# Preparing the two-part weights in the first stage instead of ahead of the experts, with stores, loads and the end put in another order

## The reference, cut to what matters

```python
# f 1, attention without softmax
h = layernorm(X, ln_w, ln_b); Q, K, V = split(h @ W_in + b_in)       # 512 -> 3 x 512
Q, K = rope(Q), rope(K)                                              # on half of the features
A = sum over tokens of (K / |K|) * V                                 # one row of 512 per sequence
Y = (A * Q) @ W_out + b_out + X
# f 2, experts: 8, the best 2 of each token, H = 256, and a shared one, 512 wide
gates = softmax of the top 2 of xf @ gate_w
routed = sum over the two of gate * (gelu(xf @ w1[e] + b1[e]) @ w2[e] + b2[e])
shared = gelu(xf @ shared_w1 + shared_b1) @ shared_w2 + shared_b2
```

## Time and profile before

| | us |
|---|---|
| median of three runs | 1025.62 |
| the profiled execution | 1027.98 |
| its span, first to last instruction | 1025.8 |
| PE / DVE / ACT / POOL busy | 896.8 / 628.3 / 442.0 / 404.4 |
| first stage, to about | 316 |
| second stage, to about | 566 |
| between, to the first expert matmul | 657.3 |
| third stage, to about | 909 |
| fourth stage, to the end | 1025.8 |

### The profile page before, as it was taken

The page is one execution under the profiler, slowest core; times in us unless marked ns, Lnnn a source line. Parts: engine busy times, 40 slices in busy tenths (PEclk is TensorE's granted clock), DMA queues, the critical chain, the costliest instruction groups (busy, mean ns, idle before and its releaser), DMA issues.

```text
span 1025.8 us, 14729 instructions
## 1 busy us (share of the span) xinstructions
PE 896.8 (87%) x4562; PEld 739.3 (72%) x4562; DVE 628.3 (61%) x1356; ACT 442.0 (43%) x830; POOL 404.4 (39%) x337
## 2 busy tenths in 40 slices
PE   1999999999997699999999748499999999969883
PEld 1877787787785467777778537488988988857662
DVE  5656766676664775656665587366665666655653
ACT  4134233433423124122242645366666666653462
POOL 3356446545631400000000000277677777730464
PEclk9999999999998889999999878799999999989886
DMA  9122644545337568645424650678778878789496
GB/s 314 45 81 105 244 143 161 188 158 200 135 144 306 190 239 312 227 165 215 154 83 169 215 151 32 238 144 149 140 147 163 154 146 149 147 176 350 62 160 107
DMA packets 78074, 174.68 MB, mean 170 GB/s; under 512 B 10841, under 2 KB 19289, under 8 KB 73137
## 3 DMA queue, kind: packets, MB, share of 16 engines
q1 hardware_dynamic: 52096, 124.60, 33.6%
q0 software_dynamic: 20592, 45.96, 25.1%
q10 hardware_dynamic: 5312, 3.18, 1.3%
HBM read 103.68 MB, written 80.53 MB: 180 GB/s over the span
## 4 chain that ended last, share of the span: by engine, by line
PE 70%; DVE 11%; issue 7%; ACT 4%; POOL 3%; DMA 2%; SPq 1%; POOLq 0%; ACTq 0%; DVEq 0%
PE bank L1434 12%; PE bank L1435 12%; PE bank L1436 12%; PE bank L1626 3%; PE bank L1628 3%; PE bank L1627 3%; PE bank L1643 3%; PE bank L1645 3%; PE bank L1644 3%; PE bank L1613 3%; PE bank L1429 3%; POOL out L1413 2%; DVE we L1061 2%; PE bank L1635 2%; ACT hb L535 1%
## 5 line engine op out<-in xcount | busy, mean ns | idle before, releaser
L1385 POOL DMA_INDIRECT f_scratch<-ro,dst x71 | 113.2, 1595 | 48.7 <-SPq L513 23.2
L1377 POOL DMA_INDIRECT xr<-n_scratch,ids x72 | 71.1, 987 | 90.9 <-issue 65.6
L1434 PE MATMUL bank<-wkv_hi,h_hi 128*128 128x512 f32 x256 | 101.1, 395 | 3.8 <-issue 3.8
L1436 PE MATMUL bank<-wkv_hi,h_lo 128*128 128x512 f32 x256 | 100.7, 393 | 0.0
L1435 PE MATMUL bank<-wkv_lo,h_hi 128*128 128x512 f32 x256 | 100.6, 393 | 0.0
L1188 DVE TENSOR_TENSOR ro<-bank,b2b 128x512 f32<-128x512 f32 x71 | 49.1, 692 | 70.3 <-PE bank L1645 70.3
L1626 PE MATMUL bank<-we,x_hi 128*128 x284 | 86.4, 304 | 0.0
L1628 PE MATMUL bank<-we,x_lo 128*128 x284 | 80.7, 284 | 0.0
L1627 PE MATMUL bank<-we,x_hi 128*128 x284 | 80.6, 284 | 0.0
L544 ACT ACTIVATE sq<-kb 128x512 f32<-128x512 f32 x32 | 20.3, 633 | 134.2 <-DVE kb L845 134.2
L1344 POOL TENSOR_TENSOR zr<-zv,half 128x4 f32<-128x4 f32 x8 | 8.1, 1009 | 137.7 <-DVE zv L961 137.7
(11 more groups left out here) (232 smaller groups left out, 2514.2 us busy)
## 6 DMA issues: line engine op xcount, KB each, us to landing
xg<-in_X SPq DMA_DIRECT2D x16, 1024.0 KB, 9.1
q_scratch<-qh SPq DMA_DIRECT2D x8, 1024.0 KB, 3.9
q_scratch<-qb SPq DMA_DIRECT2D x8, 1024.0 KB, 7.1
expert_scratch<-in_w SPq DMA_DIRECT2D x16, 512.0 KB, 7.1
q_hi<-q_scratch SPq DMA_DIRECT2D x8, 1024.0 KB, 4.7
q_lo<-q_scratch SPq DMA_DIRECT2D x8, 1024.0 KB, 6.9
out<-z SPq DMA_DIRECT2D x8, 1024.0 KB, 5.1
n_scratch<-n SPq DMA_DIRECT2D x8, 1024.0 KB, 6.4
```

The source lines that it names most:

```text
L1377: pool.indirect_dma_start(xr[u][:, :], None, n3_dram, bass.IndirectOffsetOnAxis(ids[:, i:i + 1], 0)).then_inc(row_in[u], 16)
L1385: pool.indirect_dma_start(f_dram, bass.IndirectOffsetOnAxis(dst[:, i:i + 1], 0), ro[i % NRO][:, :], None, compute_op=ALU.add).then_inc(r_s ...
L1434: pe.matmul(dst, hi(k), w_hi(k), start=(k == 0), stop=False)
L1436: last = pe.matmul(dst, lo(k), w_hi(k), start=False, stop=(k == KD - 1 and not more))
```

## The change

1. **Weights in the first stage.** The 16 expert matrices and four halves of the two shared ones are 20 "units" of 128 x 1024 (512 KB). In groups 1 to 5, four units each, a unit is loaded into one of three buffers, split by ACT (`unit_hi`) and DVE (`unit_lo`), and both parts are stored. `copy_expert` and the copies of the shared weights go.
2. **No splits later.** Experts' parts are loaded ready made (2 MB for each expert instead of 1 MB), two halves of them during steps 3 and 4. `split_s`, `split_expert`, `expert_lo` and the splits of `c1` and `c2` go.
3. **Bias row** `bo` is loaded and split at the start, and its matmul takes `ones_f` instead of `bo_one`.
4. **Fills** begin in step 1: `EARLY` is (0, 2, 4, 6, 7), and `shared_h(6)` moves into step 7. `shared_o(7, 0)` and `(7, 1)` go ahead of the batches, the other two behind the batches 2 and 5.
5. **Outputs of group six** are copied to four places of their own (`fo5` to `fo8`) and stored ahead of the later expert loads. The zeros (`zero_d`) are set at the start of the second stage, in another place, and are stored in step 2 as before.
6. **End.** `late_turn` writes four banks, all loads are ordered singly, ACT splits the turned blocks ahead of the scaling, and the last group is added to by DVE from a loaded copy of the output (`x2c`, `add_x2`) and stored by SP instead of with an adding DMA by POOL.

The diff, cut to its core:

```diff
-EARLY = (1, 3, 5, 6, 7)
+EARLY = (0, 2, 4, 6, 7)
+        units = [(e, i, 0) for e in range(E) for i in range(2)] + [(E + i, 0, h) for i in range(2) for h in range(2)]
+        UB = 3
+        w_lo = [at(f"w_lo{i}", kb_, [P, UW], F32R) for i, kb_ in enumerate((128, 132, 194))]
+        w_hi = [at(f"w_hi{i}", kb_, [P, UW], F32R) for i, kb_ in enumerate((136, 140, 176))]
-        fill = {2 + i: (("h", "o")[i % 2], EARLY[i // 2]) for i in range(6)}
+        fill = {1 + i: (("h", "o")[i % 2], EARLY[i // 2]) for i in range(7)}
...
@@ sync, first stage @@
+            def load_unit(u):
+                if u >= len(units):
+                    return
+                if u >= UB:
+                    sp.wait_ge(w_stored[u % UB], 32 * (u // UB))
+                w, k = unit_in(u)
+                sp.dma_start(w_lo[u % UB][:, :]..., w).then_inc(raw_w_in[u % UB], 16)
+            def store_unit(u):
+                sp.wait_ge(unit_split, u + 1)
+                for c, w in ((0, w_hi), (1, w_lo)):
+                    sp.dma_start(unit_out(u, c), w[u % UB][:, :]...).then_inc(w_stored[u % UB], 16)
...
             for g in range(NG):
+                u = UG * (g - 1)
+                with_units = 0 <= u < len(units)
                 sp.wait_ge(h_normed, g + 1)
                 load_x(g + 2)
+                if with_units:
+                    store_unit(u)
+                    load_unit(u + 2)
                 if g >= 1:
                     store_q(g - 1)
+                if with_units:
+                    store_unit(u + 1)
+                    load_unit(u + 3)
+                    store_unit(u + 2)
+                    load_unit(u + 4)
                 if g + 1 < NG:
                     sp.wait_ge(k_rotated, GT * (g + 1))
                     load_rt(g + 1)
+                if with_units:
+                    store_unit(u + 3)
+                    load_unit(u + 5)
...
-                if 1 <= g <= 4:
-                    copy_expert(2 * g - 2)
-                    copy_expert(2 * g - 1)
...
@@ scalar, first stage @@
+            def unit_hi(u):
+                act.wait_ge(raw_w_in[u % UB], 16 * (u // UB + 1))
+                if u >= UB:
+                    act.wait_ge(w_stored[u % UB], 32 * (u // UB))
+                act.activation(w_hi[u % UB][:, :], w_lo[u % UB][:, :]..., ACT.Copy).then_inc(unit_hi_done, 1)
                     norm_k(g, j)
                     if j == 1 and g >= 1:
                         q_hi_parts(g - 1)
+                    if 0 <= UG * (g - 1) < len(units):
+                        unit_hi(UG * (g - 1) + j)
                 if g + 1 < NG:
                     front_split(g + 1, (g + 1) % 2)
...
@@ vector, first stage @@
                 kv_prod(g, 0)
+                unit_lo(g, 0)
                 v_tile(g, 1)
                 k_tile(g, 2)
                 kv_prod(g, 1)
                 if g >= 1:
                     q_lo_parts(g - 1)
+                unit_lo(g, 1)
                 v_tile(g, 2)
                 k_tile(g, 3)
                 kv_prod(g, 2)
+                unit_lo(g, 2)
                 v_tile(g, 3)
                 kv_prod(g, 3)
+                unit_lo(g, 3)
                 rotate_q(g)
...
@@ tensor, between the stages @@
-            for m in range(KS):
-                shared_h(6, m)
             n3_turn(NG - 1)
...
                 shared_h(7, m)
+            shared_o(7, 0)
+            shared_o(7, 1)
...
-                if b in (1, 4, 7, 10):
-                    shared_o(7, (b - 1) // 3)
+                if b in (2, 5):
+                    shared_o(7, 2 + (b - 2) // 3)
...
@@ sync, after the last scatter @@
-            for n, g in enumerate(f_loads):
-                sp.dma_start(f[g][:, :, :], f_groups[g]).then_inc(f_in[n // 2], 16)
-            sp.wait_ge(stored, 16 * NT)
+            load_f(EARLY[0])
+            load_n3(1)
+            load_f(EARLY[1])
+            load_f(LATE[0])
...
+            sp.dma_start(x2c[:, :, :], out_groups[LATE[2]]).then_inc(f_in[LATE[2]], 16)
+            for j in range(GT):
+                sp.wait_ge(y_added, j + 1)
+                sp.dma_start(out_tiles[GT * LATE[2] + j], f[LATE[2]][:, j, :]).then_inc(late_stored, 16)
```

More of the change, by code:

```diff
@@ L489, in _ @@
             load_expert(2)
-            for j in range(GT):
-                store_f(6, j)
+            sp.wait_ge(t2_full, t2_use(s, KD) + 1)
             sp.wait_ge(f_stored[1], 16 * f_buf_uses[1])
-            sp.wait_ge(t2_full, t2_use(s, KD) + 1)
-            load_expert(6)
+            load_expert(6, range(2, 4))
+            sp.wait_ge(x2_stored[0], 16 * NG // 2)
+            sp.wait_ge(x2_stored[1], 16 * NG // 2)
+            sp.wait_ge(f_stored[3], 16 * f_buf_uses[3])
+            load_expert(1)
             sp.wait_ge(s_full, h_use(7, KS - 1) + 1)
@@ L497, in _ @@
             sp.dma_start(b1b[:, :, :].rearrange("p e h -> p (e h)"), b1.rearrange("e h -> (e h)").partition_broadcast(P))\
-              .then_inc(bias_in[0], 16)
-            for j in range(GT):
+              .then_inc(bias_in, 16)
+            for j in range(GT - 1):
                 store_f(7, j)
@@ L599, in _ @@
                     keep_acol(0)
+                if g == GB + 2:
+                    for u in range(UB):
+                        act.wait_ge(w_stored[u], 32 * u_uses[u])
                     scale_wo(0)
@@ L782, in _ @@
                     gelu_c(i, m)
-                for g, j in y_of[what, i, m]:
-                    normed(g, j)
                 if what == "h" and m == KS - 1 and i + 1 < len(LATE):
@@ L787, in _ @@
                         nc_hi_part(i + 1, k)
+                for g, j in y_of[what, i, m]:
+                    normed(g, j)
             normed(*y_order[-1])
@@ L1142, in _ @@
                    .then_inc(hot_marked, 1)
-                if b in (4, 7, 10, 13):
-                    f_out(7, (b - 4) // 3)
-                if b == 9:
-                    expert_lo((7,))
+                for j in {2: (0, 1), 5: (2,), 8: (3,)}.get(b, ()):
+                    f_out(7, j)
             dve.wait_ge(ids_full, 1)
@@ L1370, in _ @@
             pool.wait_ge(gates_stored, 16)
-            for u in range(3):
+            pool.wait_ge(zero_stored, 16 * (len(LATE) + 1))
+            for u in range(4):
                 pool.wait_ge(f_stored[u], 16 * f_buf_uses[u])
@@ L1554, in shared_o @@
                 n = o_use["o", g, j]
+                if g == h_order[0] and j == 0:
+                    pe.wait_ge(s_in[1], 32)
                 pe.wait_ge(hs_split, h_use(g, KS - 1) + 1)
```

338 lines of the change are left out of this document (172 added, 166 removed).

## The result

| | median of the runs, us | range | ratio to the kernel before, 95% interval |
|---|---|---|---|
| before, same chip | 1024.88 | 1023.91 to 1026.31 | |
| changed | 1040.67 | 1039.59 to 1042.88 | 1.0156 [1.0134, 1.0178] |

Slower by 16 us where 5.5 less were forecast, and outside the range (994 to 1037). The profiled execution of the changed kernel took 1039.59 us, its fastest, with a span of 1037.8; that of the kernel before took 1027.98, longer than any run in the table. So the spans are only 12.0 apart, and against the forecast 17.5 us of them are to be found.

What follows compares the result with a forecast made beforehand. PE was taken as full in the first stage (289.24 of 304 us), with later idle time behind a DVE and ACT chain holding the weight splits. -38.5 - 21 + 54 = -5.5, so 1020.1 us; range 994 to 1037.

Steps and rivals of the forecast that it cites:

- Part 1: First stage: units delay ACT's `front_split` behind a queued load; 10.7 us a group, +54 us over five groups.
- Rival C: First stage: the wait for unit u+3 is longer than forecast, time 1034 to 1041 us; chance 0.20.
- the slower access to HBM: First stage, loads behind 3 MB of stores: up to 1.8 us more a group, the kernel 9 us later.
- Part 2: Second stage: no wait for `bo`, and the turn of step 7 comes at 531.6 for 536.53, -4.9 us.
- a filled step is (536.53 - 383.78)/5 = 30.55: Second stage: six filled steps of 30.55 us each lead from 348.3 to the turn of step 7.
- the signs of being wrong: Five groups under 8 or over 12 us each, or first expert matmul not 33 to 42 us sooner without them.
- parts 2 and 3: Second stage up to the counts: -4.9 us by the turn of step 7, -18.6 in all by PE's second half.
- Part 4: Marks, lists, first tile: marks take 23.9 us, lists come 33.4 us sooner, first expert matmul 38.5 sooner in all.
- Rival D: Gathers: they wait for `store_f(7, 3)` behind 2 MB of biases, 8 us late, time 1028 us; chance 0.10.
- Part 5: The end: late products start 3.1 us sooner, run 13.8 shorter, and the tail is 4.2 shorter; -21 us.
- PE's 24 products and turns last 75.4: The end: PE's late products and turns take 75.4 us instead of 89.2, with fewer waits and cold restarts.

Runs made afterwards that it cites:

- x1: Changed kernel with 40 unread matmuls put into PE's wait in the turns of groups 2 to 6: 1032.73 us, ratio 1.0073 to the kernel before.
- e1: Changed kernel with each group's fourth unit split behind the turned blocks and Q biases (ACT) and the rotation and next statistics (DVE): 1007.57 us, ratio 0.9781.
- b2: Kernel before with three unused VectorE subtractions behind the last K-V product of groups 1 to 5: 1051.08 us, ratio 1.0203.
- e3: Changed kernel with the 4 MB of zeros issued in step 1 of the second stage instead of step 2: 1038.98 us, ratio 1.0087.
- b1: Kernel before with the 4 MB of zeros issued in step 3 of the second stage instead of step 2: 1031.99 us, ratio 1.0067.
- e4: Changed kernel with the second late group's normed rows loaded on ACT's queue instead of SP's: 1042.30 us, ratio 1.0121.
- e8: Changed kernel with one low part behind Q's, three behind the next statistics, zeros in step 1, late rows on ACT's queue: 989.18 us, ratio 0.9612.
- e5: Changed kernel with three low parts behind the last K-V product, the fourth behind the next statistics: 1005.92 us, ratio 0.9803.
- b3: Kernel before with three unused VectorE subtractions behind the next group's statistics in groups 1 to 5: 1034.99 us, ratio 1.0057.
- e2: Changed kernel with unit u+1's store and unit u+3's load issued ahead of the Q stores on SP: 1029.22 us, ratio 0.9989.

## Why the prediction was wrong

**Part 1 was right in mechanism and nearly in size.** ACT in front of `front_split`, behind a load behind stores: 11.3 us a group instead of 10.7, with waits of 9.9 to 10.5 where I had 9.1, and 1.2 or more for the clock where I had 1.6 (`x1`). The load is in 11.5 us after SP's first issue of Q (131.33 to 142.8), where I had 10.9. The period is 47.3 to 48.9, 47 was forecast. Rival C, to which I gave 0.20, asked for over 11.9 a group; it did not come. Nor does any row show the slower access to HBM that I had cited from the Trainium skill (DMA: Bandwidth & Descriptors, Latency and other measured facts) as a part of it: the first 1 MB of Q still lands 3.9 us after its issue at 131.33, as in the earlier trace rows, with the loads and stores of units around it. But the account of the wait was too simple. I followed DVE's low parts only as far as the load and called it the one cause. With the load out of the way (`e1`) 22 of the 56.5 us stay, which K tile 3 costs by being late, with the clock behind it. And I took DVE's busy time as harmless since it was not full, and each of its low parts at 1.2, where one in each group takes 2.31 beside GpSimd. `b2` shows 3.7 us a group of it, in a gap of 7 us, costing 19.9 us.

**Part 2: the step that failed is "a filled step is (536.53 - 383.78)/5 = 30.55".** I took it as the mean over five steps of the kernel before and laid it over six of the changed one. In that mean the 4 MB of zeros fell in a step with no store of f. The change brings the fills one step forward and leaves the zeros in step 2, which now holds `store_f(0, *)`. DVE waits 9.25 us for one of two buffers, PE 4.46, and the step is 37.75. That is 7.2 of the 17.5 us, and `e3` and `b1` show it from both sides. With it one of the signs of being wrong came: without the 56.5 of the first stage the first expert matmul is 27.6 us sooner, not 33 to 42. The rest of parts 2 and 3 held: the wait on `bo` gone, the next one on `q_lo` in its place (3.8 us forecast, 3.79 in the trace), the product moved out, the turn of group 7.

**Part 4 was 2.8 short.** The gates came as forecast; the marks took 25.5 us (652.41 to the lists at 677.92) where I had 23.9, and from the first gather (679.79) to the first expert matmul it was 6.5 where I had 5.6. No experiment went after this, and the cause stays open. Rival D did not occur: GpSimd's gathers start 1.9 behind the lists, as forecast.

**Part 5: the other step that failed is "PE's 24 products and turns last 75.4".** They last 86.4. I priced `n3c[1]` behind the last scatter at 0.9; it costs a wait of 5.92 in place of the 4.40 that the change removes. `e4` takes it away and gets to 83.2 (1031.1 less 947.9, by the same 8.0 behind DVE's last bank). So the other 7.8 of the 11.0 are not that load. They are short waits: PE is busy 75 us there and stands the remaining 8, most of it in waits of 1.8 to 2.3 on `hc_lo` or on issue. I had written that the change takes the wait on `hc_lo` away; it is shorter (2.16 and 2.26, one of them in place of 3.45), not gone. My figure was the busy time. Partly against it, the tail behind DVE's last bank is 8.0 us instead of 12.9. The chain of the last tile takes 5.5 (DVE's last add ends at 1035.34) where I had 4.4, but the store and the close take 2.5 and not 8.3: a plain store of 256 KB lands 2.0 us after its issue where I had 4, and no run shows the 4.3 that I put down for the program's close.

**In sum**, of 17.5 us the zeros are 7.2, the load of the late rows 3.2, the other waits of the end 7.8 less 4.9 of its tail and 1.9 ahead of it, part 4 2.8, the first stage 2.5 and the rest 1.0 (17.7 with the rounding). The zeros alone take the sum from -5.5 to about the time of the kernel before, and the end does the rest. The gains of the change without its first stage are real: 44.4 us in the trace, and `e8` keeps most of them and the corrections. A range that reached 3.7 us further would have held the time. Its upper end was built from the terms with an unknown price, while the terms that failed were those that I took as known.

## What to carry to other kernels

When work moves by one step in a software pipeline, list all that stands in the queue of each step it enters, for a mean over the old steps hides a transfer that used to fall where nobody waited. Idle time of VectorE is free only where GpSimd is idle as well and where the next thing behind it has slack; the same 3.7 us cost 20 us in one place and 3 to 6 in another. Ahead of an in-order engine's critical operation put nothing that can wait for a transfer; behind it, the same work with the same bytes was 34 us cheaper.

## What the runs showed that I had not expected

- A wait of some 3 us in each of five groups costs more than itself, for the clock falls with it: 12.6 us of waiting and 10.3 by which the same matmuls take longer in `e1`, 13.3 and 6.6 in `b2`.
- VectorE subtractions of 128x1024 take 1.22 us alone and 1.89 beside GpSimd's `h_lo`, which takes 1.91 instead of 1.27 (`e5`, `b2`); behind the statistics, where GpSimd has one operation of 128x8, they take 1.25 (`b3`).
- 40 matmuls that nobody reads, put into each of five waits, make the changed kernel 0.8% faster by ratio (`x1`). In its trace 6.0 us of that are at the first stage's end.
- A load of 0.5 MB behind 1 MB of stores lands 5.8 us after its issue, behind 3 MB 7.6 (`e2`): what is ahead in the queue has in part been moved by then, so 2 MB more cost 1.8 and not 5.6.
